# Five re-orderings in the sixth and seventh step of an adaLN block with sparse attention and a quantised linear layer

## What is computed

```
h = layernorm(x) * (1 + ca) + sa
x = x + ga * attention(h)          # 16 heads of 16 channels
h = layernorm(x) * (1 + cb) + sb
x = x + gb * ffn(h)

attention: scores = where(mask, q k^T, 0) / 4; softmax over all 512 positions; times v; out @ Wo.T + bo
           mask[i, j] is true for j = i and j = i - 2^k (10 offsets: 0, 1, 2, 4, ..., 256)
ffn:       blocks of 32 channels; scale = max(max|block| / 7.5, 1e-30)
           q = nearest value of the FP6 E2M3 grid to block / scale
           out = (q * scale) @ (same for the weight).T + bias
```

## Time and profile before

| | us |
|---|---|
| median of 3 runs | 280.79 (279.94 to 280.97) |
| profiled execution, whole launch | 280.1 |
| span of its instructions | 278.3 |
| DVE busy | 249.4 (90%) |
| PE busy, weight loads | 253.6 (91%), 162.7 |
| ACT busy | 210.8 (76%) |
| POOL busy | 209.4 (75%) |
| mean granted TensorE clock | 0.994 |

### The profile page before, as it was taken

How to read it: one execution, slowest core, us unless ns; L and a number is a source line. 1 busy time by engine, 2 the same in 40 slices (tenths; PEclk the granted TensorE clock), 3 DMA queues, 4 the chain that set the end, 5 groups by cost and what they waited for, 6 DMA issues and landing times.

```text
span 278.3 us, 4396 instructions
## 1 busy us (share of the span) xinstructions
PE 253.6 (91%) x1356; PEld 162.7 (58%) x1356; DVE 249.4 (90%) x318; ACT 210.8 (76%) x564; POOL 209.4 (75%) x159
## 2 busy tenths in 40 slices
PE   6999996999999998799999999999999578997885
PEld 1754565258636843485568654766468445895664
DVE  3699899989998999999889998999984999999970
ACT  2377896785888896989889997998776736666753
POOL 6201339996998999999999899999999899945100
PEclk9999997999999999999999999999999999999999
DMA  7752996696695489327944796069803875730006
GB/s 226 191 194 78 297 312 179 205 351 196 212 320 182 141 273 319 127 98 252 341 143 132 221 361 197 19 204 364 247 1 116 255 212 180 227 133 15 0 5 224
DMA packets 54386, 53.90 MB, mean 194 GB/s; under 512 B 4094, under 2 KB 52812, under 8 KB 54364
## 3 DMA queue, kind: packets, MB, share of 16 engines
q1 hardware_dynamic: 54364, 53.63, 60.4%
HBM read 44.89 MB, written 8.72 MB: 193 GB/s over the span
## 4 chain that ended last, share of the span: by engine, by line
DVE 32%; PE 30%; ACT 14%; POOL 13%; issue 8%; DMA 1%; DVEq 0%; POOLq 0%; ACTq 0%
POOL pv_buf L681 7%; DVE prod L1758 6%; DVE pv_buf L1894 5%; PE ps L847 5%; PE ps L1111 5%; DVE prod L1894 4%; PE ps L1032 4%; DVE prod L1747 4%; PE ps L980 3%; ACT x_norm L1217 3%; ACT dump L1240 2%; PE ps L876 2%; POOL h L394 2%; POOL x_norm L389 2%; PE ps L834 2%
## 5 line engine op out<-in xcount | busy, mean ns | idle before, releaser
L681 POOL TENSOR_TENSOR pv_buf<-pv_buf 128x1024 f32<-128x1024 f32 x48 | 113.8, 2370 | 5.0 <-DVE pv_buf L1894 0.8
L1758 DVE TENSOR_TENSOR prod<-ps,kT 128x1024 f32<-128x1024 f32 (+4 forms) x70 | 75.0, 1107 | 0.0
L1894 DVE TENSOR_TENSOR pv_buf<-v_shift,ps 128x1024 f32<-128x1024 f32 x49 | 59.0, 1209 | 1.0 <-POOL pv_buf L681 1.0
L876 PE MATMUL ps<-wT,h_cen 128*128 128x256 f32 x128 | 29.9, 379 | 0.0
L847 PE MATMUL ps<-hT,wT 128*128 128x512 f32 x64 | 29.6, 603 | 0.0
L858 PE MATMUL ps<-hT,wT 128*128 128x512 f32 x64 | 29.4, 599 | 0.0
L876 PEld LDWEIGHTS ps<-wT,h_cen 128*128 128x128 f32 x128 | 23.9, 190 | 6.4 <-issue 3.8
L980 PE MATMUL ps<-prod,sel_sum 128*32 128x512 f32 x208 | 25.0, 598 | 2.0 <-DVE prod L1758 1.5
L1032 PE MATMUL ps<-wo_g,w_raw 128*128 128x256 f32 x112 | 26.4, 379 | 0.0
L662 POOL TENSOR_TENSOR rstd<-var,minus_half 128x4 f32<-128x4 f32 x8 | 8.1, 1017 | 20.5 <-ACT var L1244 19.0
L1032 PEld LDWEIGHTS ps<-wo_g,w_raw 128*128 128x128 f32 x112 | 21.2, 190 | 3.5
(11 more groups left out here) (220 smaller groups left out, 570.7 us busy)
## 6 DMA issues: line engine op xcount, KB each, us to landing
v_shift<-v_rows SPq DMA_DIRECT2D x56, 512.0 KB, 5.5
x_in<-in_L_attn_x SPq DMA_DIRECT2D x8, 512.0 KB, 4.0
v_rows<-v_base SPq DMA_DIRECT2D x8, 512.0 KB, 3.0
x_res<-in_L_attn_x SPq DMA_DIRECT2D x8, 512.0 KB, 6.1
out_x<-outb SPq DMA_DIRECT2D x5, 512.0 KB, 4.7
rows_mod<-mod_rows SPq DMA_DIRECT2D x7, 256.0 KB, 6.1
x<-in_L_wmod SPq DMA_DIRECT2D x1, 1024.0 KB, 8.1
row_ga<-mod_rows SPq DMA_DIRECT2D x8, 128.0 KB, 3.0
```

What stands on the lines that cost most here:

```text
L681: nc.gpsimd.tensor_tensor(dst, dst, ring(b, n)[:, t:NT, :], ALU.add).then_inc(s_add, 1)
L876: mm = nc.tensor.matmul(ps23[:, k2, col:col + D], h_cen[:, k, P * t:P * t + P], wT[:, 2, k, :], start=(t % 2 == 0 and k == 0), stop=(t % 2 ...
L1758: nc.vector.tensor_tensor(prod[:, n, :, o:L], ps01[:, :, o:L], kT[:, b % 2, :, 0:L - o], ALU.mult).then_inc(s_prod, 1)
L1894: nc.vector.tensor_tensor(dst[:, at, :].rearrange("p t (h e) -> p t h e", e=DH), v_n.rearrange("p t (h e) -> p t h e", e=DH), weights, ALU ...
```

## The change

Five things are re-ordered; no instruction is added or taken away, and no shape changes.

1. POOL, sixth step: `rstd_after(4)` stands behind `add(5, 3)` instead of behind `add(5, 5)`, and `gate_projection(5)` behind `add(5, 5)` instead of behind `add(5, 7)`.
2. ACT: `norm_after(4)` stands at the end of the sixth step, ahead of `copy_scores(6)`, instead of behind `exps(6)`. `exps(6)` stands ahead of `quantised(3)`, and `evacuate_v(7, 0)` ahead of `evacuate_xd(3)`.
3. PE: `v_rows(7, 0)` stands ahead of `xd_transposes(3)`.
4. DVE, loop: `softmax_max` and `block_maxima` are cut in two. `invert_scales(b - 3)` stands between the maximum and its subtraction (b = 3, 4, 5), and the products pv 8 and pv 9 stand between the block maxima and the scales (b = 3, 4, 5).
5. DVE, seventh step: `block_maxima(4)` and `quantise(4)` stand behind `pv_product(6, 3)` instead of behind the first qk product, that is two pv products and one qk product later.

```diff
--- before.py
+++ after.py
@@ -728,17 +728,20 @@
                     gate_ffn(b - 3)
                 add(b, 2)
                 add(b, 3)
+                if not has(b + 3):
+                    rstd_after(b - 1)
                 add(b, 4)
                 add(b, 5)
                 if has(b + 3):
                     rstd_before(b + 3)
                 else:
-                    rstd_after(b - 1)
+                    gate_projection(b)
                 add(b, 6)
                 if not has(b + 3):
                     dequantise_early(b - 2)
                 add(b, 7)
-                gate_projection(b)
+                if has(b + 3):
+                    gate_projection(b)
             modulate(pool, nc.gpsimd, LAST - 3)
             gate_ffn(LAST - 4)
             add(LAST - 1, 1)
@@ -1169,8 +1172,8 @@
             q_rows(LAST, 0)
             q_rows(LAST, 1)
             v_rows(LAST, 1)
+            v_rows(LAST, 0)
             xd_transposes(LAST - 4)
-            v_rows(LAST, 0)
             attention_transposes(LAST - 2)
             v_means(means_of(LAST))
             project(LAST - 2)
@@ -1556,16 +1559,17 @@
                     take_result(b - 3, 0)
                     take_result(b - 3, 1)
 
+                if not norm1:
+                    norm_after(b - 1)
                 copy_scores(b + 1)
                 if ahead:
                     seed_q(b + 2)
 
+            exps(LAST - 1)
             quantised(LAST - 4)
-            exps(LAST - 1)
-            norm_after(LAST - 3)
             evacuate_v(LAST, 1)
+            evacuate_v(LAST, 0)
             evacuate_xd(LAST - 4)
-            evacuate_v(LAST, 0)
             evacuate_attention(LAST - 2)
             means_of_v(means_of(LAST))
             take_x1(LAST - 2, 0)
@@ -1759,13 +1763,21 @@
                                         ALU.mult).then_inc(s_prod, 1)
 
             def block_maxima(b, half_=None):
+                block_peaks(b, half_)
+                peaks_to_scales(b, half_)
+
+            def block_peaks(b, half_=None):
                 t, g, _ = halves(half_)
-                n = upto_half(b, half_)
-                src, (peak, scale, inv) = h2_by[b], block_scales(b)
+                src, peak = h2_by[b], block_scales(b)[0]
                 made, n_made = step_of(b, half_, s_h2, s_h2l)
                 dve.wait_ge(made, n_made)
                 nc.vector.tensor_reduce(peak[:, g], src[:, t, :].rearrange("p t (g k) -> p (t g) k", k=BLOCK), AX_X,
                                         ALU.max, apply_absolute_value=True).then_inc(s_post, 1)
+
+            def peaks_to_scales(b, half_=None):
+                g = halves(half_)[1]
+                n = upto_half(b, half_)
+                peak, scale, inv = block_scales(b)
                 dve.wait_ge(s_post, NPOST * n - 2)
                 if 0 < b < TAIL - 1 or b == TAIL:
                     dve.wait_ge(s_xd, b)
@@ -1832,6 +1844,9 @@
                 scores = scores_in(ps67 if b < LAST else ps23)
                 nc.vector.tensor_reduce(mx0[:, :, :], scores.rearrange("p t s h -> p t h s"), AX_X,
                                         ALU.max).then_inc(s_max, 1)
+
+            def softmax_less_max(b):
+                scores = scores_in(ps67 if b < LAST else ps23)
                 dve.wait_ge(s_max, b + 1)
                 for tiles, done in ((FIRST, s_dh), (SECOND, s_d)) if in_halves(b) else ((slice(0, NT), s_d),):
                     nc.vector.tensor_tensor(d[:, tiles, :, :], scores[:, tiles, 0:NS, :], per_head(mx0, NS)[:, tiles],
@@ -1908,6 +1923,8 @@
                 softmax_max(b)
                 if has(b - 3):
                     invert_scales(b - 3)
+                softmax_less_max(b)
+                if has(b - 3):
                     quantise(b - 3)
                 softmax_weights(b)
                 pv_product(b, 0)
@@ -1927,25 +1944,28 @@
                 if b >= 2:
                     qk(b, 8, 9)
                 pv_product(b, 7)
+                if has(b - 2):
+                    block_peaks(b - 2)
                 if b >= EARLY:
                     pv_product(b, 8)
                     pv_product(b, 9)
                 if has(b - 2):
-                    block_maxima(b - 2)
+                    peaks_to_scales(b - 2)
                 if b - 2 == TAIL - 1:
                     quantise(b - 2)
 
             b = LAST - 1
             softmax_max(b)
+            softmax_less_max(b)
             softmax_weights(b)
             pv_product(b, 0)
             pv_product(b, 1)
             qk(b, 0)
-            block_maxima(LAST - 3)
-            quantise(LAST - 3)
             pv_product(b, 2)
             qk(b, 1)
             pv_product(b, 3)
+            block_maxima(LAST - 3)
+            quantise(LAST - 3)
             qk(b, 2, 3)
             pv_product(b, 4)
             qk(b, 4, 5)
@@ -1958,6 +1978,7 @@
             pv_product(b, 9)
 
             softmax_max(LAST)
+            softmax_less_max(LAST)
             softmax_weights(LAST)
             for n in range(NO):
                 pv_product(LAST, n)
```

## The result

| | before | changed |
|---|---|---|
| median of 20 runs, us | 280.41 (279.72 to 280.99) | 281.00 (279.94 to 282.39) |
| ratio | | 1.0027, 95% interval 1.0016 to 1.0038 |
| profiled execution, us (span) | 280.1 (278.3) | 282.39 (280.5) |
| granted TensorE clock in it | 0.994 | 0.988 |

By this ratio, which goes by the means of the executions (281.13 and 280.38), the changed kernel is 0.8 us slower; the medians lie 0.6 us apart. A second measurement of the same kernel gave 1.0012 (0.9997 to 1.0027, experiment 12), which reaches down to no difference, so the size is known less well than one interval says. The forecast was 0.3 us faster, and the direction was wrong. The measured median lies inside the stated range.

A forecast was written before the change was run, and what follows sets the result against it. Waits on the path, not busy DVE or PE, bound the kernel; shifts of exponentials, POOL's last addition of batch 6 and the last variance sum to 0.3 us faster: 279.8 profiled, 280.3 predicted, range 278.5 to 282.0.

The forecast's parts named there:

- The sum up to PE's last matmuls: Shifts of the exponentials and of POOL's last addition of batch 6, putting PE's last matmuls at 242.98 to 251.44 us.
- Pairs: DVE, fifth and sixth step: the inverse ahead of the subtraction makes the exponentials 0.15 us later per step.
- Root: POOL, sixth step: the root waits for ACT's variance, so `h2` of batch 4 comes 1.12 us later, 0.82 of it new.
- PE's 74 matmuls: Last step: they follow POOL's last addition of batch 6, 0.32 us later, and end at 251.44 instead of 251.12.
- the wait for pv 2: POOL's 0.80 us wait before 218.14 goes, since DVE makes that product before the block maxima.
- The step that failed: Tail: PE's first projection half ends 0.03 us earlier and DVE's last variance starts at about 254.25 instead of 254.52.
- B: Gate row for POOL lands late, up to 6.1 us load: POOL waits 1.5, end 1.2 us later, 281.8; chance 0.13.
- A: DVE's gain of 1.3 to 2.3 us reaches the end through its last ten products: 279.3 to 278.3; chance 0.25.
- C: DVE's pairs apart gain nothing: exponentials 0.38 us later in each of two steps, 280.8, slower by 0.2; chance 0.12.

The follow-up runs named there:

- experiment 12: The changed kernel measured again, word for word; 1.0012 of before (0.9997 to 1.0027).
- port_free: Changed kernel with POOL's gated weight of batch 7 behind the root of batch 7's first half instead of ahead; 0.9988 of before.
- busy_tail: Changed kernel with five more idle matmuls on PE behind the last projection; 1.0021 of before.
- row_free: Changed kernel with POOL's dequantising of batch 4 ahead of the gated weight of batch 4; 1.0017 of before.
- experiment 11: late_port and port_free, each with POOL's gated projection weight of batch 6 moved behind its last addition of batch 6; 0.9934 and 0.9960 of before.
- the swap: The edit on POOL that puts the gated weight of batch 7 behind the root of batch 7's first half; alone on the kernel before 1.0002.
- undo_root: Changed kernel with POOL's sixth-step order and ACT's norm of batch 4 put back; 1.0001 of before.
- undo_pairs: Changed kernel with DVE's pairs put back (inverse scales behind the subtraction, block maxima together with their scales); 1.0023 of before.
- late_only: Kernel before with only the later block maxima of batch 4 in the seventh step; 0.9976 of before.
- root_only: Kernel before with only POOL's sixth-step order and ACT's earlier norm of batch 4; 1.0056 of before, 6 runs.
- port_gate: port_free with POOL's gated projection weight of batch 6 behind its last addition of batch 6; 0.9960 of before.
- experiments 2, 10: Changed kernel with root and norm put back, 1.0001; port_free with pairs put back, 0.9991, or with root and norm put back, 0.9973.
- root_port: Kernel before with POOL's sixth-step order and ACT's earlier norm of batch 4, plus the swap; 1.0019 of before.
- late_port_gate: late_port with POOL's gated projection weight of batch 6 behind its last addition of batch 6; 0.9934 of before, 6 runs.
- late_port: Kernel before with the later block maxima of batch 4 and the swap; 0.9970 of before.

## Why the prediction was wrong

**The sum up to PE's last matmuls was right.** Pairs: 0.13 for 0.15. Root: POOL waited 1.29, `h2` of batch 4 came 1.02 later for 1.12. PE's 74 matmuls start at +0.34 to +0.36 in port_free, busy_tail and row_free, for 0.32. The one mis-sized term is small: of the 0.80 that the wait for pv 2 was to give back, 0.66 came, since additions that wait for each other start some 0.14 apart anyway. That PE and POOL, not DVE's ten products, set the end is shown by experiment 11.

**The step that failed** is the last one, "PE's first half of the projection ends at 254.26 ... less 0.03, and the variance ... starts at about 254.25". I let DVE be free there and gave the shift of batch 6, which stands in front of the variance, no term in the sum. In the trace of before the shift stood where POOL's product was nearly over. The later block maxima (part 5) bring DVE there 1.1 us sooner, so that its shift now waits for POOL's scaling of batch 6 (L698), as POOL's next product does, and the two start 0.07 to 0.11 us apart. Both read two operands from SBUF, and the one that comes second takes 1.0 us longer: DVE's 2.28 and 2.27 in the changed kernel, POOL's 2.25 in busy_tail, neither in port_free. The Trainium skill has the rule on its page "SBUF — State Buffer", section "SBUF: two separate sides": a DVE instruction with two SBUF inputs and a GpSimd instruction that reads SBUF take a shared port pair exclusively, the later one waits for the whole of the other. The traces agree, from both sides. DVE's other products of the main loop read one operand from PSUM and run beside POOL's additions at an unchanged 1.13 us apart, so the trace of before has no such row; its one hint was this shift at 1.32 us, which takes 1.22 or 1.23 in the kernels with the swap.

**The price.** By executions at a clock of 0.999 or 1.000 the changed kernel has a mean of 280.6, port_free 280.1: the collision costs 0.5 us, as in the traces (variance +0.32 in row_free, -0.18 in port_free). Then comes the clock. In the experiments before had 17 of 118 executions at 0.988 (mean 281.1, the others 280.2 to 280.5), and the changed kernel, in both measurements, 12 of 31 (281.7 against 280.6 at 0.999 to 1.000). With undo_root, undo_pairs and row_free, whose profiles have the collision at 2.27 as well, it is 24 of 67. The eight kernels with the swap had 6 of 87. Of the other three without the swap, late_only had 0 of 12, busy_tail 1 of 12 and root_only 1 of 6. Roughly, and worked out with the result known: -0.3 as forecast, +0.5 collision, (12/31 - 17/118) x 1.1 = +0.3 clock, and up to +0.4 in executions with a late row: +0.5 to +0.9 for a measured 0.8.

**What stays open of the clock.** That the collision makes falls of the clock more frequent is what the counts suggest; that it does so by PE's longer pause (1.45 us for 0.92 to 0.97) is not shown. The changed kernel, undo_root and row_free have this pause and a fall behind it. But undo_pairs has the pause of 1.45 and late_only one of 1.73, and the clock does not fall there, while port_gate has the short pause of 0.92 and a fall. All five profiles at 0.988 have two falls, one near 45 us and one near 261, so 0.988 counts a second fall and does not say what brought it.

**The rivals.** B, the gate row, had the right mechanism at a quarter of its price: 0.38 in the profiled execution, 0.19 to 0.64 in three other kernels and nothing in most. A was wrong, since PE's matmuls did not start sooner. C was wrong: 0.13 a step and not 0.38. The page of the Trainium skill that the prediction set against this part, "VectorE: DVE Perf Modes", says in the same section, "The DRAIN you can't avoid", that an instruction that is not held starts earlier; the prediction left this sentence out. The traces agree with it: 1.13 us apart at 1.21 of duration, and here 0.81 at 0.89.

**Part by part, measured:** later block maxima -0.7 us (late_only); sooner root and norm +0.4 to +0.7 (experiments 2, 10 and root_port of 8), with root_only at 1.6 as the one that does not fit; pairs apart nothing that can be told; the collision +0.5 and the clock. The collision comes with part 5, not with the sum of the parts: every profile with the later block maxima and without the swap has it (2.08 in late_only, 2.27 or 2.28 in the changed kernel, undo_root, undo_pairs and row_free, on POOL's side in busy_tail), and before and root_only, which lack part 5, do not. Part 3, and the codes and the copy of v of part 2, were never put back singly, so their share is not known.

## What to carry to other kernels

When a wait goes away, look what starts next to what: two engines released by one instruction start their next ones together, and if DVE and POOL both read two SBUF operands there, one of them takes nearly as long as both (here 2.27 us for 1.23 and 1.27). Moving a short step that waits for another engine ahead of dense work costs the wait in full, unless what it feeds is really waited for: here POOL came to the modulation 1.02 us later. On an engine that runs dense to a point that others wait for, ask of each instruction whether its reader wants it before that point; moving one gated weight behind it gained 0.8 and 1.0 us, at least as much as the best of the five parts.

## What the runs showed of the hardware

- DVE and POOL instructions with two SBUF operands each, started 0.07 to 0.11 us apart: the second takes 2.25 to 2.28 instead of 1.23 to 1.27 us, whichever engine it is on. At 0.26 us apart (late_only) it takes 2.08.
- The granted TensorE clock of one kernel differs between executions in steps (0.988, 0.992 to 0.994, 0.998 to 1.000). The falls last 3.2 to 3.4 us each and lie in a few places, each behind a stretch in which PE had waited (2.53 us before 44.32 in before, 2.02 near 219.5 in late_only and late_port_gate, 0.92 to 1.46 near 257): near 45 us, where the time hardly shows it (before's executions at 0.994, with one fall in the profiled one, and at 1.000 have the same mean, 280.2), near 222, and near 261. The same waits stand in executions without a fall. The price is set by the place: 1.1 us at 261; at 222 DVE's last softmax starts 1.7 us later in late_only's profile than in late_port's, counted from batch 3's maximum.
- A DVE reciprocal of 0.35 us slipped between two dependent instructions costs 0.13: independent starts were 0.81 and 0.25 apart, the dependent one 0.93.
